# Expert matrices loaded one step earlier, FP4 block scales as a two-tensor pass, FFN residual as a product with the identity

## What is computed

```python
xn = _layernorm(x)
x = x + attn0(xn) + ffn0(xn)        # causal attention, 16 heads of 8; FFN in FP4
xn = _layernorm(x)
x = x + attn1(xn) + moe1(xn)        # attention with distance decay; 32 experts, the best 2 per token

def fp4_quant_dequant(x):           # blocks of 16 along the last dimension
    scale = max(|xb|) / 6.0
    scale = maximum(scale, 1e-12)
    xn = xb / scale
    return _GRID[searchsorted(_MID, |xn|)] * sign(xn) * scale

def ffn0(x):                        # every input and every matrix goes through fp4_quant_dequant
    h = silu(x @ w_gate.T) * (x @ w_up.T)      # 352 wide
    return h_quantised @ w_down_quantised.T

def moe1(xf):                       # W1, W2: 128 x 128 per expert
    y_e = gelu(xf @ W1[e] + b1[e]) @ W2[e] + b2[e]
    return sum over the two chosen experts of weight * y_e
```

## Time and profile before

| | us |
|---|---|
| median of 3 runs | 1206.04 |
| the runs | 1205.69, 1206.04, 1212.28 |
| the profiled execution's own time | 1211.18 |
| its span, first to last instruction | 1208.9 |
| PE busy | 937.5 (78%) |
| DVE busy | 851.6 (70%) |
| ACT busy | 604.6 (50%) |
| POOL busy | 357.7 (30%) |
| mean granted TensorE clock | 0.929 of full speed |

### The profile page before, as it was taken

How to read it: one execution, slowest core, us unless ns; L and a number is a source line. 1 busy time by engine, 2 the same in 40 slices (tenths; PEclk the granted TensorE clock), 3 DMA queues, 4 the chain that set the end, 5 groups by cost and what they waited for, 6 DMA issues and landing times.

```text
span 1208.9 us, 35271 instructions
## 1 busy us (share of the span) xinstructions
PE 937.5 (78%) x15195; PEld 508.9 (42%) x15195; DVE 851.6 (70%) x1434; ACT 604.6 (50%) x754; POOL 357.7 (30%) x421
## 2 busy tenths in 40 slices
PE   0577777778888887776787878776698988889887
PEld 0355553334444444343343334433444545455443
DVE  6789947577888888788878756455456576476726
ACT  3223221456655655553445455444356655666566
POOL 3333342203213213213030353542142423423230
PEclk9999976799989999998889889889899999999999
DMA  9600051354243244143221132034245265354217
GB/s 145 230 18 18 27 120 50 68 127 100 54 99 99 55 99 112 45 102 84 48 63 38 46 110 60 25 106 99 67 141 145 78 160 134 106 126 111 60 34 205
DMA packets 115597, 109.31 MB, mean 90 GB/s; under 512 B 13745, under 2 KB 108210, under 8 KB 115058
## 3 DMA queue, kind: packets, MB, share of 16 engines
q1 hardware_dynamic: 108370, 95.30, 31.6%
q0 software_dynamic: 7072, 11.76, 3.7%
HBM read 65.28 MB, written 48.51 MB: 94 GB/s over the span
## 4 chain that ended last, share of the span: by engine, by line
PE 41%; DVE 22%; issue 7%; ACT 6%; another core or an unknown queue 4%; SPq 2%; DMA 2%; POOL 1%; ACTq 0%; DVEq 0%; POOLq 0%
DVE a_maxes L1442 12%; PE a_psO L1225 12%; PE a_psS L1204 5%; PE a_psS L1181 5%; PE a_psS L1066 4%; ACT a_Pt L1290 4%; PE a_psM L1158 2%; PE a_psM L1164 2%; PE a_psM L1243 1%; PE a_psM L1092 1%; DVE xn L1477 1%; PE a_psS L1057 1%; DVE a_ON L1538 1%; PE a_psM L1153 1%
## 5 line engine op out<-in xcount | busy, mean ns | idle before, releaser
L1442 DVE TENSOR_REDUCE a_maxes<-a_psS 128x2 f32<-128x1024 f32 (+3 forms) x432 | 506.3, 1183 | 223.4 <-PE a_psS L1066 120.2
L1290 ACT ACTIVATE a_Pt<-a_psS 128x1024 f32<-128x1024 f32 (+1 forms) x432 | 418.2, 991 | 263.6 <-PE a_psS L1066 166.2
L1225 PE MATMUL a_psO<-a_Pt,V 128*32 128x512 f32 (+3 forms) x2048 | 234.3, 549 | 2.4 <-ACT a_Pt L1290 2.4
L1181 PE MATMUL a_psS<-K,Q 60*64 60x512 bf16 (+3 forms) x2048 | 183.0, 364 | 62.9 <-ACT a_Pt L1290 38.1
L1204 PE MATMUL a_psS<-Q,K 63*64 63x512 bf16 (+3 forms) x2048 | 183.8, 366 | 47.8 <-DVE a_maxes L1442 36.9
L1066 PE MATMUL a_psS<-dist,alpha_eye 64*64 64x128 bf16 x5120 | 170.3, 222 | 7.4 <-issue 7.4
L1066 PEld LDWEIGHTS a_psS<-dist,alpha_eye 64*64 64x64 bf16 x5120 | 140.8, 111 | 65.8 <-issue 18.5
L309 POOL TENSOR_TENSOR qkf<-qkf,parts 128x512 f32<-128x512 f32 x32 | 37.0, 1157 | 339.7 <-ACT parts L1267 337.6
L1204 PEld LDWEIGHTS a_psS<-Q,K 63*64 63x64 bf16 x2048 | 59.2, 106 | 170.3 <-DVE a_maxes L1442 78.2
L1181 PEld LDWEIGHTS a_psS<-K,Q 60*64 60x64 bf16 x2048 | 61.8, 111 | 113.2 <-ACT a_Pt L1290 58.4
L1581 POOL DMA_INDIRECT y<-spare,r_sent_id x64 | 61.6, 962 | 125.0 <-ACT spare L1321 56.4
(11 more groups left out here) (233 smaller groups left out, 1247.9 us busy)
## 6 DMA issues: line engine op xcount, KB each, us to landing
stack<-parts SPq DMA_DIRECT2D x192, 128.0 KB
expert_w<-in_expert_w SPq DMA_DIRECT2D x96, 128.5 KB
Q<-stack SPq DMA_DIRECT2D x64, 192.0 KB
K<-stack SPq DMA_DIRECT2D x64, 192.0 KB
xs<-in_c_no_token SPq DMA_DIRECT2D x24, 258.0 KB, 5.7
slots_flat<-xs SPq DMA_DIRECT2D x24, 258.0 KB
xnT<-xnT_dram SPq DMA_DIRECT2D x16, 256.0 KB, 3.1
slots_flat<-y SPq DMA_DIRECT2D x16, 256.0 KB, 4.8
```

Source lines behind the costliest of these rows:

```text
L1181: pe.matmul(banks[HEAD_ROWS * hf:HEAD_ROWS * (hf + 1), b, x * w:(x + 1) * w], Q[rows, k % 4, q, at:at + HEAD_ROWS], K[rows, k % 4, q, 0:w] ...
L1225: m = pe.matmul(psO[32 * j:32 * (j + 1), q0:T], V[:, (k - 2) // 2 % 2, kt, r, j, :], Pt[:, (nB.at(k) + unit) % RING, h % 2, x // 2 * w:(x ...
L1290: act.activation(Pt[:, u % RING, :, 0:w], psS[:, place_of["B", u] % BANK_PAIRS, :, 0:w], ACT.Exp).then_inc(p_ready, 1)
L1442: dve.tensor_reduce(maxes[:, k % 2, i, :, heads[0] // 2:heads[0] // 2 + pairs], src, AX, ALU.max, negate=True).then_inc(a_free, 1)
```

## The change

Three edits:

1. `quant_scales`: the instruction at L327, a TENSOR_SCALAR (SBUF tensor, two constants), becomes a SCALAR_TENSOR_TENSOR whose second operand is an SBUF tensor `least` filled with the least scale; one memset of 128x88 at the start fills it, and its semaphore is waited for once. All 17 quantisations use it.
2. The residual of the FFN: PE adds x into `f_ps_d` by one more matmul per tile (identity times x, 4 per sequence, after the 12 of the down product), and `s10` leaves DVE; ACT copies `f_ps_d` into `n.x` (`add`), between its two pairs of SiLUs, one turn after the down product. `project`'s places on ACT are renumbered to stand where they stood.
3. The 12 value loads and DMAs of the first experts' matrices are issued at the end of step 22 in place of the end of step 23; the waits and the row loads stay at the end of step 23.

```diff
@@ -320,11 +320,11 @@
...
-def quant_scales(dve, v, am, sc, rs, sem, base):
+def quant_scales(dve, v, am, sc, rs, least, sem, base):
...
     dve.wait_ge(sem, base + 1)
-    dve.tensor_scalar(sc, am, float(np.float32(1.0 / 6.0)) * UP, float(np.float32(1e-12)) * UP, ALU.mult, ALU.max).then_inc(sem, 1)
+    dve.scalar_tensor_tensor(sc, am, float(np.float32(1.0 / 6.0)) * UP, least, ALU.mult, ALU.max).then_inc(sem, 1)
     dve.wait_ge(sem, base + 2)
...
@@ -380,6 +380,7 @@
...
         st = n.sb("bn", [P, TILES, 6], ctx=c)
+        least = n.sb("f_least", [P, HW // BLK], ctx=c)
         dm, m2, sd = (n.sb("bn_" + x, [P, TILES], ctx=c) for x in ("dm", "m2", "sd"))
...
@@ -414,6 +415,7 @@
...
         x_loaded = [n.sem(f"x_loaded{q}", c) for q in range(4)]
+        least_set = n.sem("least_set", c)
         STATS = TILES + 8
...
@@ -513,7 +515,7 @@
...
                     quant_scales(dve, blocks(buf[w + "v"][:, p]), buf[w + "am"][:], buf[w + "sc"][:],
-                                 buf[w + "rs"][:], S[w + "_grid"], QUANT_STEPS * b)
+                                 buf[w + "rs"][:], least[:, 0:buf[w + "sc"].shape[1]], S[w + "_grid"], QUANT_STEPS * b)
...
@@ -544,26 +546,23 @@
...
-                def s10(b, p):
-                    dve.wait_ge(S["down"], b + 1)
-                    xv = n.x[:, b * NT:(b + 1) * NT, :]
-                    dve.tensor_tensor(xv, ps_d[:], xv, ALU.add).then_inc(S["added"], 1)
-
                 for s in range(2):
...
                 m.then_inc(w_zeroed, 1)
+                dve.memset(least[:], float(np.float32(1e-12)) * UP).then_inc(least_set, 1)
                 dve.memset(n.ones[:], 1.0)
...
                 dve.wait_ge(w_zeroed, 1)
+                dve.wait_ge(least_set, 1)
                 dve.wait_ge(w_loaded, 16 * 7)
-                quant_scales(dve, blocks(w), w_am, w_sc, w_rs, w_gridded, 0)
+                quant_scales(dve, blocks(w), w_am, w_sc, w_rs, least[:, 0:W // BLK], w_gridded, 0)
                 quant_grid(dve, w, w_rs, wt, wu, w_gridded, 0)
...
                 statistics()
-                run_ffn_steps([(0, sh), (1, sm), (-1, s10), (2, sx), (1, sm_rest)])
+                run_ffn_steps([(0, sh), (1, sm), (2, sx), (1, sm_rest)])
                 dve.wait_ge(memsets, 1)
...
@@ -592,6 +591,10 @@
...
+                def add(b, p):
+                    act.wait_ge(S["down"], b + 1)
+                    act.activation(n.x[:, b * NT:(b + 1) * NT, :], ps_d[:], ACT.Copy).then_inc(S["added"], 1)
+
                 def a10(b, p):
...
@@ -600,9 +603,10 @@
...
-                def project(it, which):
-                    if it != SEQS - 2 or which > 2:
+                def project(it, at):
+                    if it != SEQS - 2 or at not in (0, 2, 3):
                         return
+                    which = (0, 2, 3).index(at)
                     act.wait_ge(n.misc_ready, which + 1)
...
@@ -631,7 +635,7 @@
...
                 act.activation(sd[:], m2[:], ACT.Sqrt).then_inc(sd_ready, 1)
-                run_ffn_steps([(1, a5), (1, a5_rest), (0, a10), (2, a1_rest)], project)
+                run_ffn_steps([(1, a5), (-1, add), (1, a5_rest), (0, a10), (2, a1_rest)], project)
...
@@ -744,8 +748,9 @@
...
                             r = P if q < 2 else rem
-                            m = pe.matmul(ps_d[:, i, :], hqT[0:r, q, i * P:(i + 1) * P], wdT[0:r, q, :],
-                                          start=(q == 0), stop=(q == FFC - 1))
+                            pe.matmul(ps_d[:, i, :], hqT[0:r, q, i * P:(i + 1) * P], wdT[0:r, q, :],
+                                      start=(q == 0), stop=False)
+                        m = pe.matmul(ps_d[:, i, :], n.ident[:], n.x[:, b * NT + i, :], start=False, stop=True)
                     m.then_inc(S["down"], 1)
...
@@ -1024,9 +1029,10 @@
...
                         load_attention_weights(n, sp, 1)
-                    if k == EXPERT_STEPS[0] - 1:
+                    if k == EXPERT_STEPS[0] - 2:
                         for e in range(STEP_GROUPS):
                             load_weights(e, e * GROUP)
+                    if k == EXPERT_STEPS[0] - 1:
                         sp.wait_ge(misc_free, find_misc(SCATTER_STEPS[2], ("CB", SEQS - 1)) + 1)
...
```

## The result

| us | before | after |
|---|---|---|
| median | 1205.87 (4 runs) | 1190.36 (4 runs) |
| the runs from, to | 1201.19, 1212.28 | 1186.90, 1194.44 |
| span of the profiled execution | 1208.9 | 1192.6 |
| mean granted clock | 0.929 | 0.941 |

The ratio is 0.988, with a 95% interval from 0.984 to 0.992: 15.5 us faster, where -5.8 us and a range from 1193 to 1207 us were forecast. The direction was right, the size was not, and the range was too narrow.

What follows compares the result with a forecast made beforehand. No single bound: SP's issuing held PE at step 24, DVE set the FFN turns. Edits 3, 1 and 2 summed as -9.7 + 0 + 3.9 = -5.8 us, taking 1206.0 to 1200.2 us, range 1193 to 1207.

Steps and rivals of the forecast that it cites:

- PE's side of edit 2: FFN down products: 8 more PE instructions per sequence, uncovered in some turns and the tail; +3.9 us, bounds +2 and +6.
- the low clock behind the hole of edit 3: Step 24, PE's work after the idle wait: full clock would gain 1.5 us at most; 0.8 taken.
- Edit 3, -9.7 us: Step 24: matrices issued a step earlier remove PE's whole 8.89 us wait for rows, plus 0.8 of clock; -10.4 to -5.5.
- B: Step 24: the hole only shrinks because the last scatter lands later; -1.0 us, 1205.0 us; chance 0.09.
- D: Step 24: moving the matrices does nothing because the rows wait for something else; +3.9 us, 1210 us; chance 0.02.
- Edit 1, 0 us: Scales' pass L327: with two SBUF inputs it still waits for POOL's pass and ends with it; gain 0.
- Rival A: FFN turns: the two-tensor scales' pass is spared POOL's wait; -11.3 us in all, 1194.7 us; chance 0.10.
- Edit 2, DVE's side: FFN: DVE's 0.67 us addition is hidden in L327's wait for POOL; removal gains only in the turn after 73.77.
- the tail: Last FFN down product, passes in a row at low clock: the 8 extra PE instructions cost +1.65 us.
- The first two pieces: Extra PE work in the turn ending at 73.77 (+0.8 us) and the turn with 0.60 us of room (+0.4).
- the turn with the projections: FFN turn ending at 153.90, bound by PE: the extra instructions cost +1.0 us.
- Rival C: FFN: PE at low clock becomes the bound of the whole FFN, slower by +9 us, 1215 us; chance 0.04.

Runs made afterwards that it cites:

- f1: All three edits again, against the kernel before on another chip: 1133.50 us against 1147.45, ratio 0.989.
- g3: All three edits a third time, against the kernel before: 1189.37 us against 1200.77, ratio 0.990.
- g1: Only the matrix loads moved, yet one step earlier than in the change, against the kernel before: 1189.95 us against 1200.77, ratio 0.991.
- e3: Only the scales' pass with the SBUF tensor `least`, against the kernel before: 1202.68 us against 1199.67, ratio 1.002.
- f3: The change without the scales' pass edit (earlier loads and residual on PE), against the kernel before: 1136.04 us against 1147.45, ratio 0.988.
- e4: Kernel before plus 8 PE products per down product (identity times zeros), addition left on DVE: 1201.86 us against 1199.67, ratio 1.003.
- f2: The kernel before, unchanged, run again to measure scatter: 1146.67 us against 1147.45, ratio 1.000.
- f4: The change without the residual on PE (earlier loads and scales' pass), against the kernel before: 1136.06 us against 1147.45, ratio 0.989.
- e1: Only the matrix loads moved one step earlier, against the kernel before: 1193.32 us against 1199.67, ratio 0.994.
- g2: Only the matrix loads moved one step earlier, measured a second time, against the kernel before: 1189.94 us against 1200.77, ratio 0.992.
- e2: Only the residual moved to PE with the ACT copy, against the kernel before: 1201.04 us against 1199.67, ratio 1.001.
- g4: Scales' pass and residual on PE, loads left where they were, against the kernel before: 1202.04 us against 1200.77, ratio 1.003.

## Why the prediction was right or wrong

Of the 9.7 us between the forecast's -5.8 and the measured -15.5, two mis-sized terms hold 4.7: PE's side of edit 2, charged with +3.9 and about +0.5 in the traces, and the low clock behind the hole of edit 3, taken as 0.8 where about 1.9 went (the idle time itself was 0.2 us more). The other 5 us are in no term of the sum, and their cause stays open. The repeats of the whole change gave -14.0 us (f1) and -11.4 (g3) by the medians.

**Edit 3, -9.7 us: the mechanism was right, the term too small by 1.3 us.** The wait of 8.89 us is gone, the rows were ready before PE came (1.3 us to spare were forecast), and rivals B and D fall. At their new place the matrices used up the 1.2 us of room in SP's queue (they end at 808.38 us, the maxima follow at 808.42), but that cost nothing that shows: g1, with the matrices a step further out, is no faster. The term that was mis-sized is the clock: I took 0.8 of "a gain of 1.5 at most". Measured is -11.0, of which the idle time is 9.1 on average (8.89 in the first trace), so about 1.9. The windows give nearly as much: 4.00 us of work at 0.55 or, in the trace before, 0.59 of the full clock are 1.8 and 1.6 us lost,

```profile
850.98:854.98 4.00, 4.00 (x41) 1.89 (x42) 1.99 (x3) 1.02 (x1) 0.00 (x0) 0.59 0.53 131
```

and PE is busy all the time there, so nothing of it is hidden. I had halved it because "DVE and ACT lose the pause in which they caught up"; the measured 1.9 us leave nothing for that pause.

**Edit 1, 0 us: confirmed, but for 0.05 us a turn.** L327 takes 1.22 us beside POOL's pass of 2.59, and alone, at another place of the same trace, 0.19:

```profile
73.46 0.19 DVE L327 SCALAR_TENSOR_TENSOR f_xsc<-f_xam,f_least 128x32 f32<-128x32 f32 x1
```

This agrees with the Trainium skill ("SBUF — State Buffer", Who interferes with whom): two SBUF inputs contend with a GpSimd instruction that reads SBUF. The old form, with one SBUF input, waited just as long (1.21 us in the earlier trace rows), so the runs show that the new form is not spared, not that its second input is the reason. e3 measured +3.0 us with an interval that includes 0, and f1, which has edit 1, is 2.5 us below f3, which has not, by the medians and 0.2 by the means, with 4 us of uncertainty. Rival A falls. It was probably also priced too high: with edit 2 in place a spared L327 would let L339, which has two SBUF inputs itself, start while POOL's pass still runs. That is argued from the order of the passes; no run shows it.

**Edit 2, DVE's side: confirmed.** In the ordinary turns L327 ends 2.7 us after L346 with and without the addition. "Only in the turn after 73.77" was right as well: that is the turn from the second to the third down product, and it is 0.54 us shorter without the addition (f1 against e4), where 0.67 were forecast.

**Edit 2, PE's side, +3.9 us: the term that failed most.** Its largest pieces took the clock of one execution as a property of the place: 4.57 us for the first down product, which took 2.94 in the six other traces without the extra work, and 32 instructions at low clock throughout in the tail. The first two pieces (+1.2 together) came to +0.3 us, the turn with the projections (+1.0) to +0.4, the tail (+1.65) to +0.9. Measured are +1.4 us to the attention's start, perhaps -0.9 behind it, where the sum had no term, and nothing in the medians of g3 against g2. Rival C fell with it: up to the projections the longest turn with the residual's product is 16.1 us (f3, g3), and without it 17.7 (f2, f4).

**The base.** 1206.04 us was the median of three executions. Over 35 and 28 executions on two chips where it is about as fast, the same kernel has 1199.67 and 1200.77. With -11.0 and +0.5 us, from 1200 us, the changed kernel would stand at 1189.5; measured are 1190.36 and, in g3, 1189.37. That would put 5 us of the miss into the base, carried as if it were exact. It is not shown: of those 63 executions six reach 1205.69 us, which three of the first four did, so plain scatter explains the high base badly, and nothing else was tried. The range also does not follow from its own terms. A landing wait of twice 4.13 us leaves 2.85 us of the hole, which is -6.0 and not -5.5; and the bounds from rival A's 1194.7 to 1206.5 us, widened by half of the spread on either side, are 1191 to 1210 us and not 1193 to 1207. The measured time lies outside both.

**What stays open.** The whole change has ratios 0.988, 0.989 and 0.990, the load without the residual's product (e1, g1, g2, f4) 0.994, 0.991, 0.992 and 0.989. The difference of the means, 0.3%, is as large as one interval's half-width. e1's 0.994 is itself open: its interval just misses the -11.0 us of the step marks, which its own trace shows (44.79 us). Whether edit 2 gains 2 us or so beside edit 3, by the clock behind the FFN, these runs don't settle; without edit 3 (e2, g4) it gained nothing. No version was faster than the changed kernel by more than the uncertainty. Whether the scales' pass would be spared with `least` in PSUM was not tried.

## What to carry to other kernels

In a queue that issues in order, put a long run of issues (here 12 at 1.08 us each) where the queue would wait anyway, and keep in front of a load only what that load needs; what an idle hole costs is its length plus the low clock behind it, here 9.1 and about 1.9 us. A small pass that waits for another engine's pass hides the passes in front of it, so removing one of those gains nothing where that other pass ends no earlier (here the addition's 0.67 us, in all turns but those in which DVE was late). Before pricing a term by the granted clock of one trace, ask whether the place has that clock in every execution; with a scatter of 10 us over executions, the time between two marks on either side of the edit tells more than the median does.

## What the runs showed of the hardware that I had not expected

**The chip matters more than the change.** The same kernel has 1200 us on two chips and 1147 us on the third. From the mark of step 20 to that of step 24 it is 161.9 us in the first trace and 128.0 in f2, from step 25 to step 32 265.9 and 248.0; up to step 20 only 5.4 us lie between them. From step 20 on POOL issues indirect transfers. At the start of their second half, in the first trace, five scatters went out back to back, and from the sixth on each waited some 3 us for a maxima pass of DVE

```profile
758.49 0.97 POOL L1568 DMA_INDIRECT xs<-slots_flat,slots  x1 [0.30 <-issue]
759.77 0.97 POOL L1568 DMA_INDIRECT xs<-slots_flat,slots  x1 [0.30 <-issue]
763.56 0.96 POOL L1568 DMA_INDIRECT xs<-slots_flat,slots  x1 [2.83 <-DVE a_maxes L1442]
767.60 0.97 POOL L1568 DMA_INDIRECT xs<-slots_flat,slots  x1 [3.07 <-DVE a_maxes L1442]
```

and in f2 seven went out back to back before one waited, for 1.31 us:

```profile
741.63 0.97 POOL L1568 DMA_INDIRECT xs<-slots_flat,slots  x1 [0.30 <-issue]
742.90 0.97 POOL L1568 DMA_INDIRECT xs<-slots_flat,slots  x1 [0.30 <-issue]
744.18 0.97 POOL L1568 DMA_INDIRECT xs<-slots_flat,slots  x1 [0.30 <-issue]
746.46 0.97 POOL L1568 DMA_INDIRECT xs<-slots_flat,slots  x1 [1.31 <-DVE a_maxes L1442]
```

The steps around them got shorter with it. Whether the scatters are the cause or only follow was not tried. The edit's gain was nearly the same on that chip: 10.1 us between the marks, from one trace without it, against 10.9 in the e and g groups.

**The granted clock differs from one execution to the next.** g1 and g2 have the same instructions up to the attention and ran on the same chip. From POOL's first pass to the attention's first product g1 took 153.5 us and g2 149.7, and the opening behind it 20.4 and 17.4. From 4 to 8 us behind the first product the granted clock was 0.60 in g1 and 1.00 in g2:

```profile
186.55:190.55 4.00, 3.15 (x22) 0.99 (x26) 3.81 (x5) 0.05 (x1) 0.00 (x0) 0.60 0.00 0
```

```profile
183.05:187.05 4.00, 2.31 (x27) 0.82 (x27) 4.00 (x6) 1.08 (x2) 0.06 (x1) 1.00 0.00 0
```

Of the 16.3 us between the first two traces at the mark of step 32, about 5 were of this kind: from POOL's first pass to the mark of step 1 the trace before took 174.5 us where its seven average 171.1, and the trace after 170.3 where its six average 171.6.
